# Eight cores, a cumulative mean and slot routing: a smaller descriptor ring, a third weight slot, seven weight groups by way of DRAM, and a two-pair transpose buffer with another order of the stream

## What is computed

```python
# 1: causal mean of the normalized rows, normalized, added
x = x + _layernorm(softmax(causal zeros) @ _layernorm(x))       # = cumulative mean over rows
# 2: slots. u = _layernorm(x); S is a constant [64, 1024]
h = gelu(concat(u, mean(S)) @ w1 + b1)
logits = (h @ w2 + b2) / (abs(tau) + 0.1)
alpha = softmax over the 8 largest of 64, zero elsewhere         # [4096, 64]
si = (alpha.T @ u) / (alpha.sum over rows + 1e-8)                # [64, 1024]
gi = si @ Wih.T + bih ; gh = S @ Whh.T + bhh                     # 3 gates of 1024
r, z = sigmoid(gi_r + gh_r), sigmoid(gi_z + gh_z); n = tanh(gi_n + r * gh_n)
S_new = (1 - z) * n + z * S
q, k, v = S_new @ wq, S_new @ wk, S_new @ wv                     # wq, wk: 1024 x 256
y = layernorm(S_new + softmax(q @ k.T / 16) @ v)
out = alpha @ (y @ wvp + bvp) @ wo + bo
x = x + _layernorm(out)
```

## Time and profile before

| what | us |
|---|---|
| median of 3 runs (320.13 to 321.61) | 321.55 |
| the profiled execution's own time | 320.65 |
| its span on the slowest core (core 7) | 319.1 |
| spans of the eight cores | 312.9 to 319.1 |
| stream, to the end of `siT` (DVE L658) | 0 to 208.1 |
| middle, to the first matmul of the output | 208.1 to 266.75 |
| output | 266.75 to 319.1 |

### The profile page before, as it was taken

How to read it: one execution, slowest core, us unless ns; L and a number is a source line. 1 busy time by engine, 2 the same in 40 slices (tenths; PEclk the granted TensorE clock), 3 DMA queues, 4 the chain that set the end, 5 groups by cost and what they waited for, 6 DMA issues and landing times.

```text
span 319.1 us, 5787 instructions; the slowest of 8 cores (312.9 to 319.1 us)
## 1 busy us (share of the span) xinstructions
PE 225.5 (71%) x1806; PEld 130.5 (41%) x1806; DVE 198.1 (62%) x358; ACT 178.1 (56%) x332; POOL 165.2 (52%) x236
## 2 busy tenths in 40 slices
PE   0033763995998989969799778963758892888720
PEld 0000333672775767747676477620233330111100
DVE  0378935798787897898955654420222403999970
...
DMA  6999999999999996999999981599999300999998
GB/s 158 262 233 171 171 211 234 258 258 236 249 229 268 236 198 86 137 128 155 112 115 95 110 126 35 75 248 204 180 315 264 75 0 0 361 341 350 351 366 339
DMA packets 24784, 63.33 MB, mean 198 GB/s; under 512 B 1926, under 2 KB 2438, under 8 KB 24754
## 3 DMA queue, kind: packets, MB, share of 16 engines
q0 software_dynamic: 11376, 22.22, 50.1%
q1 hardware_dynamic: 12576, 40.18, 38.0%
...
## 4 chain that ended last, share of the span: by engine, by line
PE 34%; DMA 24%; DVE 17%; ACT 14%; issue 7%; POOL 1%; DVEq 0%; ACTq 0%; SPq 0%; POOLq 0%
PE R L369 9%; DVE sb_x L867 9%; DMA x3b_s<-w1b 9%; DMA wsl<-wbf 8%; DMA sb_x<-x 6%; PE R L534 4%; ACT junk L338 3%; ACT junk L323 2%; PE R L353 2%; PE R L309 2%; ACT x1b L859 2%; PE R L314 2%; PE R L473 2%; PE R L453 2%; ACT L436 2%
## 5 line engine op out<-in xcount | busy, mean ns | idle before, releaser
L369 PE MATMUL R<-xT,w1a_s 128*128 128x256 bf16 x512 | 65.7, 277 | 1.1 <-DVE Lb L415 1.1
L369 PEld LDWEIGHTS R<-xT,w1a_s 128*128 128x128 bf16 x512 | 50.9, 100 | 11.4 <-issue 2.3
L346 POOL TENSOR_SCALAR x3b_s<-sb_x,nm,vr 128x1024 bf16<-128x1024 f32 x32 | 38.4, 1201 | 12.8 <-PE R L453 4.3
L334 DVE SCALAR_TENSOR_TENSOR sb_x<-R,sqs,sb_x 128x1024 f32<-128x1024 f32 x32 | 40.7, 1272 | 5.9 <-POOL sqs L331 5.9
L338 ACT ACTIVATE junk<-sb_x,nm 128x1024 bf16<-128x1024 f32 x32 | 36.5, 1140 | 10.4 <-DVE sb_x L334 10.4
L867 DVE SCALAR_TENSOR_TENSOR sb_x<-R,sqs,sb_x 128x1024 f32<-128x1024 f32 x32 | 38.9, 1283 | 3.3 <-POOL sqs L865 3.3
L300 POOL TENSOR_SCALAR x1b<-sb_x,nm,r 128x1024 bf16<-128x1024 f32 x32 | 39.1, 1226 | 1.6 <-POOL r L294 1.3
L323 ACT ACTIVATE junk<-R 128x1024 bf16<-128x1024 f32 x32 | 32.5, 1015 | 10.5 <-PE R L319 10.0
L851 PE MATMUL R<-svd,aT 64*128 64x512 bf16 x64 | 29.5, 582 | 11.5 <-DVE sb_x L867 8.9
L859 ACT ACTIVATE x1b<-R 128x1024 bf16<-128x1024 f32 x32 | 32.7, 1023 | 5.3 <-PE R L851 2.1
L309 PE MATMUL R<-x1b,cmat 128*128 128x512 bf16 x60 | 19.9, 417 | 20.1 <-DVE sb_x L334 18.4
...
## 6 DMA issues: line engine op xcount, KB each, us to landing
...
sb_x<-x SPq DMA_DIRECT2D x15, 1024.0 KB, 24.9
wbf<-wmid POOLq DMA_DIRECT2D x6, 1024.0 KB, 18.8
sb_x<-whh POOLq DMA_DIRECT2D x4, 1024.0 KB, 52.7
wsl<-wmid POOLq DMA_DIRECT2D x4, 1024.0 KB, 14.5
msl<-wbf SPq DMA_DIRECT2D x4, 1024.0 KB, 21.1
wsl<-whh POOLq DMA_DIRECT2D x2, 1024.0 KB, 87.7
msl<-wmid POOLq DMA_DIRECT2D x2, 1024.0 KB, 16.8
```

Source lines behind the costliest of these rows:

```text
L334: kx2[j] = DV.put(lambda v: v.scalar_tensor_tensor(xs(j), RR[j % 2][:], s2[:, j:j + 1], xs(j), op0=OP.mult, op1=OP.add), ks2[j], kx1[j])
L346: kx3[j] = PO.put(lambda g: g.tensor_scalar(x3s(j), xs(j), nm[:, j:j + 1], r3[:, j:j + 1], op0=OP.add, op1=OP.mult), t, kx2[j], ksi.get(j ...
L369: PE.quiet(lambda e, jc=jc, dc=dc, ob=ob, q=q: e.matmul(ob, w1a[:, dc * H + jc * P:dc * H + (jc + 1) * P], xT[:, dc * 2 * P:(dc + 1) * 2 * ...
```

## The change

1. The SBUF area for the descriptors of POOL's DMAs shrinks from 16 KB of a partition (the default) to 4 KB.
2. `wsl` has three slots (`NW` = 3), so there are seven slots and groups 0 to 6 have one each. Group 2 has the new slot and is loaded at i = 6. Group 3 takes the slot in `x1b`. Groups 4, 5 and 6 go to `msl`.
3. Group 7 is cast too; the casts stand at i = 7, 8, 11, 12, 13, 14 and 15.
4. Only the two DMAs of Whh for gate r are issued at the start, those for z at i = 0 and those for n at i = 2.
5. The load of tiles 8 and 9 waits for `w1a` in place of `w1b`; that of 10 and 11 waits for `w1b`.
6. `xT` holds two pairs, and `evac_t` waits for the hidden matmuls of two pairs ago.
7. `ORDER` is another. The even tile's `make_x2` stands in the middle of the iteration and the odd tile's at its end, `weigh` is an iteration later, both gelus are an iteration later and `hidden_b` goes before `hidden_a`. `gate_h` stands behind `gelu_b`.
8. `last_h`, for which the fetch of the first `msl` slot waits, is now `khA`.

```diff
-NW = 2
+NW = 3
...
 ORDER = [
-    ("make_x2", -1), ("trans", -3), ("logits", -3), ("sq_c", 0), ("slot_in", -10), ("slot_in", -9),
...
+    ("sq_c", 0), ("trans", -3), ("make_x1", 1), ("scale2", 0), ("gelu_b", -3), ("weigh", -4),
...
-    nc = bass.Bass("TRN2", target_bir_lowering=False)
+    nc = bass.Bass("TRN2", target_bir_lowering=False, dynamic_dma_scratch_size=4096)
...
-        xT = sba("xT", [P, 8 * 2 * P], BF16)
+        xT = sba("xT", [P, 2 * 8 * 2 * P], BF16)
...
-        load_x(8, 2, kw1b)
-        for a in range(10, 24, 2):
+        load_x(8, 2, kw1a)
+        load_x(10, 2, kw1b)
+        for a in range(12, 24, 2):
             load_x(a, 2)
...
+        load_whh(0)
...
-                            kT[j], khA.get(j // 2 - 1), khB.get(j // 2 - 1))
+                            kT[j], khA.get(j // 2 - 2), khB.get(j // 2 - 2))
...
-        CAST_AT = {7: (4,), 9: (5,), 11: (6,), 12: (8,), 13: (10,), 14: (11,)}
+        WHH_AT = {0: 1, 2: 2}
+        CAST_AT = {7: (4,), 8: (5,), 11: (6,), 12: (7,), 13: (8,), 14: (10,), 15: (11,)}
...
+            if i in WHH_AT:
+                load_whh(WHH_AT[i])
+            if i == 6:
+                tw[2] = group("wm", slot(2), wmid_d[2])
...
             if i == 10:
-                for g in range(NW):
+                for g in range(2):
                     tw[g] = group("wm", slot(g), wmid_d[g], tt["slots"])
...
+                if name == "gelu_b" and i in GATE_AT:
+                    g = GATE_AT[i]
+                    t = gate_h(g, BB, kgB[n])
...
-        last_h = khB[NP - 1]
+        last_h = khA[NP - 1]
```

More of the change, by code:

```diff
@@ L47 @@
 ORDER = [
-    ("make_x2", -1), ("trans", -3), ("logits", -3), ("sq_c", 0), ("slot_in", -10), ("slot_in", -9),
-    ("make_x3", -2), ("evac_t", -3), ("top", -3), ("stats", 6), ("cumsum", 1), ("sq_x", -1),
-    ("scale2", 0), ("hidden_a", -2), ("shift", -3), ("exps", -3), ("sq_c", 1), ("hidden_b", -2),
-    ("make_x3", -1), ("stats", 7), ("gelu_a", -2), ("scale2", 1), ("trans", -2), ("make_x1", 3),
-    ("gelu_b", -2), ("make_x1", 4), ("make_x2", 0), ("cumsum", 2), ("weigh", -3), ("sq_x", 0),
-    ("evac_t", -2),
+    ("sq_c", 0), ("trans", -3), ("make_x1", 1), ("scale2", 0), ("gelu_b", -3), ("weigh", -4),
+    ("gelu_a", -3), ("slot_in", -10), ("cumsum", 1), ("stats", 6), ("evac_t", -3), ("sq_x", -1),
+    ("make_x2", 0), ("logits", -3), ("top", -3), ("make_x3", -2), ("shift", -3), ("sq_c", 1),
+    ("slot_in", -9), ("hidden_b", -2), ("make_x3", -1), ("sq_x", 0), ("scale2", 1), ("stats", 7),
+    ("exps", -3), ("make_x1", 4), ("trans", -2), ("cumsum", 2), ("evac_t", -2), ("hidden_a", -2),
+    ("make_x2", 1),
 ]
@@ L265, in _build, with load_whh @@
         kw2 = gdma("w2", w2[:], w2_d)
-        load_x(8, 2, kw1b)
-        for a in range(10, 24, 2):
+        load_x(8, 2, kw1a)
+        load_x(10, 2, kw1b)
+        for a in range(12, 24, 2):
             load_x(a, 2)
-        kwh = {g: [group("whh", whh_at[g][:, u * GC * D:(u + 1) * GC * D], whh_d[g, u]) for u in range(2)]
-               for g in range(3)}
+        kwh = {}
+        def load_whh(g):
+            kwh[g] = [group("whh", whh_at[g][:, u * GC * D:(u + 1) * GC * D], whh_d[g, u]) for u in range(2)]
+        load_whh(0)
         t = DV.put(lambda v: v.tensor_reduce(smf[:], sT[:].rearrange("p (c s) -> p c s", s=NS),
@@ L370, in hidden @@
                         ob, w1a[:, dc * H + jc * P:dc * H + (jc + 1) * P],
-                        xT[:, dc * 2 * P:(dc + 1) * 2 * P], start=(q == 0 and dc == 0), stop=False,
+                        xT[:, (8 * (i % 2) + dc) * 2 * P:(8 * (i % 2) + dc + 1) * 2 * P], start=(q == 0 and dc == 0), stop=False,
                         skip_group_check=True), kxT[2 * i], kxT[2 * i + 1], kw1a, *need)
```

22 lines of the change are left out of this document (10 added, 12 removed).

## The result

The changed kernel is **slower by 0.57%**: its time over that of the kernel before is 1.0057, with a 95% interval of 1.0031 to 1.0082, or 1.8 us. By the ratio 321.55 us become 323.4. That lies inside the forecast's own 318.6 to 323.7, but the sign is wrong, and the size is right by luck: three large terms cancel.

The account below looks back on a forecast made before the run. DMA waits after siT were taken to bound the kernel: POOL's queue (206.4 to 211.5), plus 10.4 and 7.6 to spk, plus 6.5, put L750 at 236.0 instead of 237.24. So 321.55 - 1.2 = 320.3 us, range 303 to 327.

Parts of the forecast that it names:

- the 81.9 us behind L750: From q/k's first matmul on group 6 to the end: no wait for a weight, so left unchanged at 81.9 us.
- The stream: Tile iterations up to siT: the new order saves 5 us, between -3 and 9, putting siT at about 203.
- The start: First tiles: the 5.46 us wait for tile 8 goes; 0 to 5 us gained, counted as 1 within the stream's 5.
- POOL's queue: POOL's DMAs through group 3: one more cast (9.6) and group 3 (7.6) end it at 206.4 to 211.5 us.
- `spk` and q/k: Middle after the stream: spk lands at 227.8 to 232.9, L750 6.5 later at 234.3 to 239.4, taken as 236.0.
- rival 1: Middle: SP's loads pass POOL's backlog, L750 at 217.2, 301.5 us, or 305 to 316 with half; chance 0.20, 0.10 in part.
- Later weights (7 to 12) land before they are needed: Behind spk: 20 us of DMA work remain, to 248, while the first matmul on group 11 is 23 us after L750.
- The 15 us at most: Middle: without DMA waits L750 could start 14.2 after siT instead of 29.1, 15 us that the forecast left unremoved.
- Rival 2: Middle: group 12 gets ahead of spk, L750 at 238.1 to 243.2, say 241, so 325.3 us; chance 0.20.
- Rival 3: Start: the 4 KB descriptor area fills and POOL stands still, first tile 20 us later, 335 us or more; chance 0.07.
- Rival 4: The stream gets slower, by up to 3 us; unseen at the end unless siT comes after about 214; no chance given.
- The range: Whole kernel, 8 in 10: 303 to 327 us; the forecast's own, from L750 at 234.3 to 239.4, 318.6 to 323.7.

Follow-up runs that it names:

- slot_late: The changed kernel with one ORDER entry moved, the first slot_in of an iteration now behind cumsum, logits and top; 1.0081 of the kernel before.
- only_weights: The changed kernel with the ORDER of the kernel before and the places of gates, constants and weight sum belonging to it; 1.0148 of the kernel before (325.4 us).
- after: The changed kernel itself, with no further edit; 1.0057 of the kernel before.
- only_order: The kernel before with the new ORDER, its gate and constant places, the two-pair xT and a 12 KB descriptor area; 1.0137 of the kernel before.
- hold_later: The changed kernel with groups 9 and 12 issued only when group 8 has landed; 0.9867 of the kernel before (316.5 us).
- new_hold6: The changed kernel with group 11 loaded straight, not cast, and groups 9, 11 and 12 held until group 8 has landed; 0.9756 of the kernel before.
- oldw_hold6: The changed kernel with the old ORDER, group 11 not cast, and groups 9, 11 and 12 held until group 8 has landed; 0.9577 of before (308.19 us).
- oldw_hold: The run only_weights with groups 9 and 12 issued only when group 8 has landed; 0.9945 of the kernel before (320.4 us).

## Why the prediction was wrong, step by step

Two steps failed. The one that made the changed kernel slower and not faster is a term put at nothing, that the 81.9 us behind L750 hold no wait for a weight and stay as they are: they grew by 6.4 us in the median (95.2 us on core 4), since v waits for group 8. The other is the stream, taken as 5 us shorter and measured 7.4 longer; beside seven casts this cost no time (slot_late). Between them the sum put L750 itself 1.2 us earlier, and it came 6.6 earlier in the median (232.4 to 225.8).

- **The stream: wrong by sign, and the cause named as the risk.** I took 5 us off, with a loss of 3 as the other end; measured are 7.4 more. 5 to 6 of it are the pace (126.8 for 120.9), by `slot_in` waiting for `weigh` of its own iteration and by the clock behind these waits. The prediction named this wait and then bounded it by a feeling that full engines give back what they gain. It could have been priced: `weigh` stood two entries ahead of `slot_in` in the new table, on another engine, five instructions long, with all of PE's work of the iteration queued behind it. What spreading `weigh`, `exps` and `shift` was to gain is not seen in any run. That PE's clock falls behind a wait of 3 to 4 us was not in the sum at all.
- **The start.** The wait for tile 8 is gone as forecast, and in only_weights the 8th tile is 2.8 us earlier than before. In after it is 1.3 later (64.0 for 62.7). The two edits together lose what each alone gains (only_order 61.3), and the rows show where. With the new table DVE waits for POOL's `scale2` (L336) at two early `make_x2`, core 4 of after:

```profile
25.86 1.28 DVE L339 SCALAR_TENSOR_TENSOR sb_x<-R,sqs,sb_x 128x1024 f32<-128x1024 f32 x1 [5.59 <-POOL sqs L336]
45.73 1.28 DVE L339 SCALAR_TENSOR_TENSOR sb_x<-R,sqs,sb_x 128x1024 f32<-128x1024 f32 x1 [3.26 <-POOL sqs L336]
```

In only_order these two waits are 4.03 and 1.87. Just ahead of each POOL now issues two DMAs of Whh (at 22.44 for 1.54 us and at 42.32 for 1.55), and the two waits are longer by 1.56 + 1.39 = 2.95 us, close to the 2.7 between the two kernels. The old table (only_weights) has neither wait. The sum had the four DMAs as 2.98 us, but not the order in which they cost it.

- **POOL's queue: right.** Group 3 lands at 209.6 (core 4), inside the 206.4 to 211.5 worked out from a cast of 9.6 and a straight load of 7.6; in only_weights, whose `siT` is the forecast's, it lands at 213.5 in the median, the 213 that I had named. (One reading was off and changes nothing: the 87.7 us of the two last DMAs of Whh are their median, and the later one lands at 108.5, not at 102.9.) It was issued at 191, not near 181, and as `siT` came at 212, gate z did not wait for it. The 5 us of stream that were "worth nothing" when gained also cost nothing when lost: slot_late gives 5.9 back and the time stays. In only_order, where group 3 lands before the stream ends, the later stream did cost, 4.4 us.
- **`spk` and q/k: the sum fits the stream that it assumed, and the stream was another.** For `siT` at 203 it gave 234.3 to 239.4 for L750. only_weights has `siT` at 202.4 and q/k at 233.2 in the median, 239.4 on its slowest core. In after, group 9 was issued (216.09) after `spk` (211.51) and when two of the three loads ahead of `spk` had landed, so most of its 7.6 us were not ahead of `spk`; `spk` landed at 220.5, below the 222 that I had named as the mark of rival 1. Yet rival 1 is not what happened: POOL's queue had run empty at 209.6, while the stream went on.
- **"Later weights (7 to 12) land before they are needed": wrong, and the step that made it slower.** I counted 20 us of transfers behind `spk` and compared the last of them with L750 + 23. I should have asked it of each group: 8 is needed some 6 us after q/k starts. The wait is 2 to 8 us on seven of eight cores, and the stretch gives back 6.4 of the 14.7 us won; hold_later changes nothing else, has no such wait and gains about 1.9% on after.
- **The 15 us at most: right as a figure.** q/k at 13.7 after `siT` in after, 12.9 in new_hold6, 14.2 in oldw_hold6, against the 14.2 worked out. I took them for not to be had.
- **The rivals.** Rival 2 (group 12 ahead of `spk`) had no room: group 12 was issued at 219.11, 1.4 before `spk` landed. Its mechanism did happen, with group 9 ahead of group 8. Rival 3 did not occur: each of POOL's DMA instructions lasts 0.8 us, as at 216.09 above, so 4 KB held all that was outstanding. That was less than I had counted: by issues and landings at most 207 descriptors of an engine, at i = 0, and 198 at i = 2, not 240, since w1b had landed by then. The estimate of 256 worked out from the Trainium skill (DMA: Bandwidth & Descriptors, Terms, and SWDGE vs HWDGE vs iDMA) stands uncontradicted, but nothing here comes near enough to test it. Rival 4 was held harmless unless `siT` came after 214: at 212.1 that was nearly tested, and slot_late says that it was harmless.
- **The range** held, and the forecast's own as well, but by luck: -14.7 in the middle met +7.4 before and +6.4 behind it.

What stays open: why the cores of one execution lie so far apart (304.6 to 321.3 us in after; group 3 at 210 on one core and 223 on another in only_weights), and why the seventh cast costs 12 us in oldw_hold and not 9.6 + 3.2 less 7.6. No run was made with a part of the cores idle.
